# A four-layer triangle kernel: the turned picture written by GpSimd's addition, stored without gaps, and plane stores from a second queue

## What is computed

```python
x = x + conv0(gn(x))        # layer 0: einsum 'bikd,bjkd->bijd' in bfloat16
x = x + conv1(gn(x))        # layer 1: einsum 'bikc,bjkc->bijc' in float32
x = x + conv2(gn(x))        # layer 2: einsum 'bkjd,bkid->bijd' / n
x = x + conv3(gn(x))        # layer 3: einsum 'bkjd,bkid->bijd'

def conv(x):                # the common form
    xn = layer_norm(x)                        # over the 64 channels (not in layer 3)
    left  = (xn @ Wl + bl) * sigmoid(xn @ Wlg + blg) * mask
    right = (xn @ Wr + br) * sigmoid(xn @ Wrg + brg) * mask
    gate  = sigmoid(xn @ Wog + bog)
    t = einsum(left, right)                   # contraction over one picture axis, per channel
    return (layer_norm(t) * gate) @ Wo + bo   # in layers 1 and 3 the gate comes after the product
```

## Time and profile before

| | us |
|---|---|
| median of 3 runs | 1504.13 (1502.86 to 1506.29) |
| the profiled execution, its own time | 1509.19 |
| its span, first to last instruction | 1507.0 |
| TensorE busy | 1283.4 (85%) |
| VectorE busy | 1015.5 (67%) |
| ScalarE busy | 935.8 (62%) |
| GpSimd busy | 534.9 (35%) |
| DMA queue q1, share of 16 engines | 53.7% |

### The profile page before, as it was taken

The page is one execution under the profiler, slowest core; times in us unless marked ns, Lnnn a source line. Parts: engine busy times, 40 slices in busy tenths (PEclk is TensorE's granted clock), DMA queues, the critical chain, the costliest instruction groups (busy, mean ns, idle before and its releaser), DMA issues. The chain is left out here.

```text
span 1507.0 us, 43585 instructions
## 1 busy us (share of the span) xinstructions
PE 1283.4 (85%) x12934; PEld 788.4 (52%) x12934; DVE 1015.5 (67%) x2928; ACT 935.8 (62%) x2045; POOL 534.9 (35%) x490
## 2 busy tenths in 40 slices
PE   0799998699789998989970799999789788899898
PEld 0455554377544444765540566667455344467555
DVE  6577774268789997217980588851299899921587
ACT  0577774389677775228970688851399677722575
POOL 0355551035456554003540566630056300000355
PEclk9899999789999999999995899999999899999999
DMA  8011113458633332796659333339788544469798
GB/s 279 21 54 47 52 47 101 117 164 256 203 96 104 104 107 78 233 289 178 191 146 210 114 115 115 115 109 300 232 247 275 189 153 152 152 194 314 210 295 258
DMA packets 206501, 249.31 MB, mean 165 GB/s; under 512 B 29024, under 2 KB 196320, under 8 KB 206432
## 3 DMA queue, kind: packets, MB, share of 16 engines
q1 hardware_dynamic: 206432, 248.42, 53.7%
HBM read 139.83 MB, written 108.53 MB: 165 GB/s over the span
## 5 line engine op out<-in xcount | busy, mean ns | idle before, releaser
L1016 DVE SCALAR_TENSOR_TENSOR lr<-ps,mask,act_out 128x128 f32 (+5 forms) x1152 | 279.2, 311 | 53.3 <-ACT act_out L763 47.0
L1185 POOL TENSOR_TENSOR rstd<-ve,half_col 128x6 f32<-128x6 f32 x144 | 190.5, 1323 | 257.3 <-DVE ve L983 223.6
L1230 POOL TENSOR_TENSOR new_ring<-val,lr 128x384 f32<-128x384 f32 x96 | 103.2, 1075 | 396.9 <-issue 311.9
L528 PE MATMUL ps<-w_parts,val 64*128 64x256 bf16 (+1 forms) x1728 | 199.9, 310 | 19.0 <-DVE lr L1016 18.0
L763 ACT ACTIVATE act_out<-ps 128x384 f32<-128x384 f32 x384 | 176.0, 483 | 51.0 <-PE ps L538 34.1
L1218 POOL TENSOR_TENSOR val<-act_out,gate_ring 128x384 f32<-128x384 f32 x96 | 109.8, 1144 | 246.0 <-ACT act_out L838 208.3
L804 ACT ACTIVATE in_ring<-ps 128x768 f32<-128x768 f32 (+1 forms) x64 | 51.9, 811 | 189.7 <-PE ps L596 145.8
L815 ACT ACTIVATE cen<-ps 128x384 f32<-128x384 f32 x192 | 109.3, 569 | 73.2 <-PE ps L638 73.1
L739 ACT ACTIVATE cen<-ps,gn 128x384 f32<-128x384 f32 x144 | 83.8, 582 | 101.8 <-PE ps L483 99.2
L638 PE MATMUL ps<-in_ring,k 128*128 128x384 f32 x288 | 131.3, 540 | 13.6 <-DMA in_ring<-t_scratch 13.1
L596 PE MATMUL ps<-lr 64*128 64x192 f32 (+3 forms) x896 | 129.2, 335 | 12.9 <-DVE lr L1016 5.2
(11 more groups left out here) (110 smaller groups left out, 2691.2 us busy)
## 6 DMA issues: line engine op xcount, KB each, us to landing
gate_scratch<-gate_ring SPq DMA_DIRECT2D x192, 192.0 KB, 2.3
gate_ring<-gate_scratch SPq DMA_DIRECT2D x96, 384.0 KB, 3.7
in_ring<-x_scratch SPq DMA_DIRECT2D x144, 192.0 KB, 2.4
lr<-x_scratch SPq DMA_DIRECT2D x72, 384.0 KB, 4.6
in_ring<-t_scratch SPq DMA_DIRECT2D x144, 192.0 KB, 3.3
x_scratch<-new_ring SPq DMA_DIRECT2D x48, 384.0 KB, 3.2
t_scratch<-in_ring SPq DMA_DIRECT2D x48, 384.0 KB, 3.4
lr<-x SPq DMA_DIRECT2D x6, 1536.0 KB, 16.0
```

Source lines behind the costliest of these rows:

```text
L528: mm = nc.tensor.matmul(banks[h][:, :, 0:P], moving(x, s)[half(h), N * r:N * r + P], proj_weights(w, h)[:, 0:2 * P], start=start, stop=sto ...
L1016: ins = nc.vector.scalar_tensor_tensor(out5[:, h, lo // 2:hi // 2, :, m], ps[:, 4 + 2 * r + h, lo:hi].rearrange("p (a e) -> p a e", e=2), ...
L1185: nc.gpsimd.tensor_tensor(rstd[:, s % 2, :], ve[:, s % 2, :], half_col[:, :], ALU.pow)\
```

## The change

In five parts:

1. *Turning.* `turned` moves to the upper 48 slots of `lr`. GpSimd's addition in layer 1 writes `turned` directly, with elements 384 bytes apart; ScalarE's `turn` is gone, and VectorE's `bn_stats` of layer 1 reads `turned` with the same spacing.
2. *Its store.* A new DRAM tensor `turned_scratch` of shape [2, 2, 64, 96, 96] takes it without gaps. SP stores the first 8 columns of each half (`EARLY = 4`), ScalarE's queue the other 88: four DMAs each, of 64 partitions.
3. *Layer 2's loads.* `gather` loads pairs of tiles from it, two DMAs per pair whose runs in SBUF are 96 floats; `keep` stores each loaded pair to `x_scratch` in natural order for the residual. So tiles are in natural order and the centring and the finishing are one instruction each. VectorE waits for the turned store just ahead of the first `glu`.
4. *Planes.* Four plane buffers instead of two (two in `in_ring`, `xn`, `act_out`; tails in four slots of `cen`), and ScalarE issues the main part's store right behind its own copy. Layer 0's first gate loads move from B1 to B2. Residuals lie in slots 0 to 47 in all layers.
5. *Start of B2.* ScalarE spreads tile 0 before the deviation of tile 1; VectorE's order is adapted; TensorE gets two more `keep_clock` products there.

```diff
@@ top
-EARLY = 8
+EARLY = 4
@@ names
-        turned = lr[:, 0:N * HALF].rearrange("p (j i) -> p j i", i=HALF)
+        turned = lr[:, N * HALF:2 * N * HALF].rearrange("p (j i) -> p j i", i=HALF)
+        def turned_tile(n):
+            return turned[:, :, bass.ds(ROWS * n, ROWS)].rearrange("p j i -> p i j")
+        def turned_rows(h, h2, first, behind):
+            return (turned_dram[h, h2, :, first:behind, :],
+                    turned[C * h:C * h + C, HALF * h2 + first:HALF * h2 + behind, :])
@@ SyncE, phase A
+                def gather(n, s):
+                    for h in range(2):
+                        rows = turned_dram[h].rearrange("h2 c j i -> (h2 c) j i")[:, bass.ds(ROWS * n, 2 * ROWS), :]
+                        slot = in_ring[:, s:s + 2, :].rearrange("p a (r i) -> p (a r) i", r=ROWS)
+                        sp.dma_start(slot[:, :, HALF * h:HALF * h + HALF], rows).then_inc(in_loaded[s], 16)
+                def keep(n, i, s):
+                    sp.wait_ge(in_loaded[s], in_count(l) + 32 * (i + 1))
+                    sp.dma_start(two_tiles(scratch, n), in_ring[:, s:s + 2, :]).then_inc(natural_stored[s // 2], 16)
+                if l == 2:
+                    for n in range(0, RING, 2):
+                        gather(n, n)
+                    for n in range(0, RING, 2):
+                        keep(n, 0, n)
+                    sp.wait_ge(turned_stored[1], 16 * 4)
+                    for n in range(0, RING, 2):
+                        sp.wait_ge(used, l * TILES + n + 2)
+                        sp.wait_ge(natural_stored[n // 2], 16)
+                        gather(RING + n, n)
+                    keep(RING, 1, 0)
+                    over_tiles(sp, step_gathering, 2 * RING)
+                    return
@@ SyncE, phase B1
-                    sp.dma_start(dram[g, 0:P, :, :], main).then_inc(planes_stored[g % 2], 16)
@@ SyncE, end of layer 1's phase B2
-                    sp.wait_ge(b2_turned, TILES)
+                    sp.wait_ge(b2_new, (l + 1) * TILES)
+                    for h2 in range(2):
+                        for h in range(2):
+                            sp.dma_start(*turned_rows(h, h2, 0, ROWS * EARLY)).then_inc(turned_stored[0], 16)
@@ TensorE
-                    for z, x in zip(column_parts(l, ps[:, s % 2, 0:TILE]),
-                                    x_parts(l, in_ring[:, s, :]) if l else [x_all[:, n, :]]):
-                        mm = nc.tensor.matmul(z, w_centre[:, :], x, start=True, stop=True)
+                    nc.tensor.matmul(ps[:, s % 2, 0:TILE], w_centre[:, :], in_ring[:, s, :] if l else x_all[:, n, :],
+                                     start=True, stop=True).then_inc(a_z, 1)
@@ ScalarE, phase B1
-                    if g >= 2:
-                        act.wait_ge(planes_stored[g % 2], 48 * (l * (GROUPS // 2) + g // 2))
+                    if g >= RING:
+                        act.wait_ge(planes_stored[g % RING], planes_count(l, g))
...
+                    act.wait_ge(b1_main, l * GROUPS + g + 1)
+                    act.dma_start(plane_dram(l)[g, 0:P, :, :], main).then_inc(planes_stored[g % RING], 16)
@@ ScalarE, phase B2 of layer 1
-                    turn(TILES - 1, RING - 1)
+                    act.wait_ge(b2_new, (l + 1) * TILES)
+                    for h2 in range(2):
+                        for h in range(2):
+                            act.dma_start(*turned_rows(h, h2, ROWS * EARLY, HALF)).then_inc(turned_stored[1], 16)
@@ VectorE, phase A (the wait now stands behind low(0, 0), ahead of over_tiles)
-                if l == 2:
-                    for part in range(2):
-                        dve.wait_ge(turned_stored[part], 16 * 4)
@@ VectorE, phase B2
+                    new = turned_tile(n) if l == 1 else new_ring[:, s, :]
+                    nc.vector.bn_stats(stats[:, n, :], new).then_inc(stats_done, 1)
@@ GpSimd, residual
                     if l == 1:
-                        slot_free(pool, b2_turned, n - RING + 1)
-                        slot_free(pool, stats_done, (l + 1) * TILES + n - RING + 1)
+                        nc.gpsimd.tensor_tensor(turned_tile(n), rows(val[:, s % 2, :]), rows(residual_slot(l, n)),
+                                                ALU.add).then_inc(b2_new, 1)
+                        return
```

137 lines of the change are left out of this document (68 added, 69 removed).

## The result

| | before | after |
|---|---|---|
| median, us | 1504.06 (1502.86 to 1506.29, 4 runs) | 1482.12 (1480.34 to 1487.17, 4 runs) |
| ratio | | 0.9858, 95% interval 0.9831 to 0.9885 |
| profiled execution: own time, span | 1509.19, 1507.0 | 1481.32, 1479.5 |

The account below looks back on a forecast made before the run. Seen as bounds: the turned store between layers 1 and 2, full engines in phase B2, and layer 0's plane copies waiting for stores. Terms summed to -27.2 from the 1504.1 us median, giving 1477 us, range 1452 to 1497.

Parts of the forecast that it names:

- Layer 0's B1, -12.5: Layer 0's phase B1: with four buffers plane copies follow TensorE at 1.65 us a group; -12.5 us, bounds -14 and -8.
- B1 of layers 1 to 3, -3.7: Phase B1 of the float32 layers: the last plane copies no longer wait for stores; -3.7 us, bounds -4 and 0.
- Layer 1's B2, +17: Layer 1's phase B2: bn_stats reading elements 384 bytes apart costs VectorE 0.35 us more, 48 times; +17 us, bounds 0 and +26.
- The step for GpSimd: Layer 1's B2: GpSimd's scattered addition goes from 1.04 to 1.5 us, covered by its idle time; cost 0.
- the rival of a GpSimd bound: Layer 1's B2: GpSimd's scattered write sets the pace and the kernel is slower, 1531 us; chance 0.07.
- Turned store and layer 2's start-up, -15: Joint of layers 1 and 2: layer 2's start-up, 13.2 us, runs under the turned store, at 213 GB/s; -15 us.
- The rival of ScalarE's late stores taking the engines: Joint: early store and gathers land only when the late store does, so the -15 is lost, 1492 us; chance 0.17.
- That 64 partitions limit the store: Turned store: reading 64 partitions, not gaps, limits its rate to 206 to 214 GB/s, for the new stores too.
- Handovers -4: Handovers to B2: 0.7 us each in layers 1 to 3, about 2 us in layer 0's constant products; -4 us.
- start of B2 -2: Start of B2: tile 0's spreading waits about 1 us less per layer, half eaten by added products; -2 us, bounds -4, +3.
- Layer 2's B2, -6: Layer 2's B2: one finish of about 0.6 us replaces two of 411 ns; -6 us, bounds -3 and -9.
- Its phase A, -1: Layer 2's phase A: one centring product instead of two halves, five DMAs per two tiles; -1 us, bounds -6 and +6.

Follow-up runs that it names:

- e5_two: The change with two plane buffers for B1 instead of four, ScalarE still issuing the main store: 1492.24 us, ratio 0.9892 to the kernel before.
- e6_sp: The change with SP issuing each plane group's main store again, four plane buffers kept: 1493.55 us, ratio 0.9905 to the kernel before.
- e1_pairs: The change with layer 1's bn_stats walking the turned tile as it lies, in pairs of neighbouring elements: 1471.02 us, ratio 0.9758 to the kernel before.
- e2_runs: The change with the turned store's DRAM side padded, so that its runs are 1,536 bytes: 1476.62 us, ratio 0.9785 to the kernel before.
- e3_order: The change with ScalarE issuing the late store only after the early store and first gathers have landed: 1477.60 us, ratio 0.9817 to the kernel before.
- e12_best: The change with e1_pairs' and e3_order's edits, the late store divided by partition halves between ScalarE and SP: 1457.13 us, ratio 0.9676 to the kernel before.
- e13_one: The change with e1_pairs' and e3_order's edits and a DRAM layout letting each late-store DMA take all 128 partitions: 1452.43 us, ratio 0.9640 to the kernel before.
- e0_after: The change run again without edits; its table gives stage lengths over profiles of unchanged code: 1485.96 us, ratio 0.9851 to the kernel before.
- e7_start: The change with the old order of B2's start in all layers, without the two added keep_clock products: 1497.43 us, ratio 0.9936 to the kernel before.
- e4_undo: The change with turning back on ScalarE, GpSimd writing and bn_stats reading the natural tile: 1471.60 us, ratio 0.9753 to the kernel before.

## Why the prediction was right, and where it was not

The time fell inside the range, but that the total came so close is in part luck: three terms were off, and their errors cancelled. Term by term:

- **Layer 0's B1, -12.5: right** (-12.1). Mechanism and pace held: 24.4 us from the first copy to the last, 1.62 us a group against 1.65. e5_two and e6_sp show that the buffers and the second queue each carry part of it. That the size came out to 0.4 us is partly luck, since unchanged code took 25.7 to 29.4 us for this stage.
- **B1 of layers 1 to 3, -3.7: right in size** (-2.5, -0.8 and -0.4). The mechanism is shown: with two buffers (e5_two) the last copies wait for stores again and 1.4, 0.4 and 0.6 us come back. With SP's issue and four buffers (e6_sp) nothing does, so here it was the buffers alone.
- **Layer 1's B2, +17: right mechanism, mis-sized.** The step took ScalarE's +0.35 us a tile; `bn_stats` measured +0.29, of which 11.6 us show in the stretch, since VectorE had a little room. It reads scattered single elements at a price, and e1_pairs removes all of it. By the rule of the Trainium skill, *Advanced Engine Details and Errata*, SBUF Cachelines, two hits on a 16-byte line are wanted; 838 ns at one element a line and 544 at two agree for VectorE's reads; GpSimd's writes at one element a line showed no such price (1,070 ns against 1,036). The step for GpSimd took the same ratio and 1.5 us: it was 1.07. A price taken from ScalarE's scattered writes fitted VectorE's scattered reads and not GpSimd's scattered writes; the rival of a GpSimd bound never came near.
- **Turned store and layer 2's start-up, -15: wrong, the step failed that has "early stores and gathers that land around 798".** That is on the time base of before, 14 us behind its last `bn_stats` (783.9). In the change the early store landed at 806.6, 40 us behind the last `bn_stats` (766.8), and the gathers after it: layer 2's first product came at 813.59, 2 us behind the late store's landing, and the start-up followed the store as it had before. The store itself went as forecast or a little faster (229 GB/s with SP's part in it, against 213). The rival of ScalarE's late stores taking the engines is what happened: its mechanism, one short packet for each of 2.6 us, is in the packet counts (256 and 256), and two cures that share nothing but the mechanism (e2_runs by the run's length, e3_order by the order) took 11.2 and 6.2 us off the joint. Only 2.9 of the 15 us came. The Trainium skill, *DMA: Bandwidth & Descriptors*, Queues, rings and completion order, has engines go round the queues by packets; the equal counts agree, and here one run of 33,792 bytes was one packet. The 8 us for which ScalarE's packets stood back in e12_best are not explained by it.
- **That 64 partitions limit the store: right**, read from a single stretch of the earlier trace rows and shown by e13_one (205 against 423 GB/s). The Trainium skill, *SBUF — State Buffer*, Door 1, says so too. The prediction built on it for the new stores as a given; it was the largest gain open in this kernel, about 18 us of joint.
- **Handovers -4 and start of B2 -2: both mis-sized**; together they measured -7.0 in layer 0, -3.9 in layer 1, -2.0 in layer 2 and -0.9 in layer 3 (and -5.5, -4.1, -2.4 and -1.7 by the means of e0_after's table). The constant products fell by 3.0 us in layer 0 (9.69 to 6.69), where 2 were taken; three of the ten kernels with this code had 8.38, so 1.3 to 3.0 is the fair figure. In layer 1 they fell as well, from 9.55 to 6.69, for which the sum had nothing; e5_two had 8.38 there and no longer handover, so what that gave in time stays open. The greater error was to price the order by one operation of ScalarE, "about 1 us" a layer: e7_start shows some 11 us for the four starts.
- **Layer 2's B2, -6: right**: the `finish` of 600 ns, and 4.8 us between its first and last `bn_stats`. **Its phase A, -1:** +1.5, inside the bounds.

The errors were +12 on the joint, -5 on the statistics and -8 on the starts and handovers. They cancelled, so that the profiles differ by what the sum said though three of its terms were wrong. The 5 us between 1477 and 1482 are those by which the profiled execution of before stood above its median: the terms were read from an execution slower than most, and what was saved in it is not all saved in the others.

## What to carry to other kernels

In this kernel the queues shared the DMA engines by packets, not by bytes: a large store in runs of 33,792 bytes held back another queue's small urgent one, with as many packets, for its own whole length (37.3 of 41.2 us). Short runs (10.6 us) or an explicit order cured it. Let each large DMA span all 128 partitions (here 381 to 423 GB/s against 205), even if the layout costs the reader more DMAs. When a tile is written scattered, look at who reads it back: walking it in the order of its memory was free where the natural order cost half as much again, and statistics don't mind the order.

## What was not expected of the hardware

- GpSimd's addition with every element written 384 bytes from the last took 1.07 us against 1.04 to a contiguous tile, while ScalarE's copy into the same places took 1.16 us in e4_undo, against 0.80 and 0.75 us for its other full tiles in the same stretch.
- `bn_stats` at pairs of elements 384 bytes apart took 544 ns, no more than contiguous. Contiguous, pairs and single elements are the only patterns measured.
- A packet of 33,792 bytes took 2.6 us with one half of the partitions in flight and 1.26 with both; one of 1,536 bytes 107 ns and 65 to 68. Short runs cost about 10% of the rate when all partitions are read (381 against 423 GB/s) and nothing when half are.
- In e12_best the second queue's first packets came 8 us behind their issue, as the first queue's first DMA ended; in the change they came 2 us behind it. The cause is open.
